# FFN heads with early tables, quartered centring and side-by-side gates, attention loops written out, and matmuls without a reader

## The reference

```
x = x + 0.5 * ffn(layernorm(x))
x = x + attention(layernorm(x))     # 16 heads of 32, causal
x = x + 0.5 * ffn(layernorm(x))

ffn(x):  gate = x @ Wg.T ; up = x @ Wu.T          # Wg, Wu: 4096 x 512
         out = (gelu_tanh(gate) * up) @ Wd.T      # Wd: 512 x 4096
layernorm(x) = (x - mean) / sqrt(var + 1e-5)
```

## Time and profile before

| | |
|---|---|
| median of three runs | 2982.96 us (2982.94 to 2984.21) |
| the profiled execution | 2983.2 us |
| its span, first to last instruction | 2981.4 us |
| TensorE busy | 2904.1 us (97%) |
| VectorE busy | 1826.8 us (61%) |
| ScalarE busy | 1052.5 us (35%) |
| GpSimd busy | 1069.3 us (36%) |
| mean granted clock of TensorE | 0.991 |
| packets of the instruction queue | 115, 1.88 MB |

### The profile page before, as it was taken

One profiled execution on the slowest core, in us unless ns is written; L12 is line 12 of the kernel. 1 busy time (PEld: TensorE's weight loads), 2 busy tenths in 40 slices (PEclk: granted clock), 3 DMA queues, 4 the chain that ended last, 5 costly groups with the idle time before them and its releaser, 6 DMA issues. The chain is left out here.

```text
span 2981.4 us, 51041 instructions
## 1 busy us (share of the span) xinstructions
PE 2904.1 (97%) x19280; PEld 2342.2 (79%) x19280; DVE 1826.8 (61%) x3312; ACT 1052.5 (35%) x1825; POOL 1069.3 (36%) x745
## 2 busy tenths in 40 slices
PE   6999999999999999999999999899999999999999
PEld 5888888888888878777777776678888888888887
DVE  5656665565666544576777675675656665565654
ACT  4322222222222222266666664432222222222222
POOL 3322222222222224466666663342222222222221
PEclk9999999999999999999999999999999999999999
DMA  3001000000000015722322222100000000000001
GB/s 99 27 24 29 21 28 21 21 25 25 28 21 28 1 47 113 220 72 59 71 59 63 68 75 71 39 29 22 26 25 28 21 28 21 21 24 26 28 8 57
DMA packets 98586, 127.95 MB, mean 43 GB/s; under 512 B 43020, under 2 KB 51196, under 8 KB 95100
## 3 DMA queue, kind: packets, MB, share of 16 engines
q1 hardware_dynamic: 98428, 125.72, 15.3%
HBM read 96.34 MB, written 29.34 MB: 42 GB/s over the span
## 5 line engine op out<-in xcount | busy, mean ns | idle before, releaser
L59 PE MATMUL psum<-ffn_x_high,ffn_w_high 128*128 128x512 f32 x2048 | 801.6, 391 | 16.7 <-POOL ffn_x_low L212 9.5
L60 PE MATMUL psum<-ffn_x_low,ffn_w_high 128*128 128x512 f32 x2048 | 798.0, 390 | 0.0
L61 PE MATMUL psum<-ffn_x_high,ffn_w_low 128*128 128x512 f32 x2048 | 798.0, 390 | 0.0
L589 POOL TENSOR_TENSOR ffn_inner<-ffn_gelu,ffn_inner 128x512 fp32r<-128x512 f32 x256 | 345.6, 1350 | 1169.1 <-ACT ffn_inner L527 1169.1
L434 DVE SCALAR_TENSOR_TENSOR ffn_gelu<-ffn_gelu,psum 128x512 f32<-128x512 f32 x256 | 176.0, 687 | 604.1 <-ACT ffn_gelu L520 604.1
L59 PEld LDWEIGHTS psum<-ffn_x_high,ffn_w_high 128*128 128x128 f32 x2048 | 385.0, 188 | 105.4 <-POOL ffn_x_low L212 10.0
L61 PEld LDWEIGHTS psum<-ffn_x_high,ffn_w_low 128*128 128x128 f32 x2048 | 385.0, 188 | 80.1
L60 PEld LDWEIGHTS psum<-ffn_x_low,ffn_w_high 128*128 128x128 f32 x2048 | 385.2, 188 | 79.0
L59 PE MATMUL psum<-ffn_inner,ffn_w_high 128*128 128x512 f32 x1024 | 398.6, 389 | 0.2
L60 PE MATMUL psum<-ffn_inner,ffn_w_high 128*128 128x512 f32 x1024 | 398.4, 389 | 0.0
L61 PE MATMUL psum<-ffn_inner,ffn_w_low 128*128 128x512 f32 x1024 | 398.4, 389 | 0.0
(11 more groups left out here) (120 smaller groups left out, 3520.5 us busy)
## 6 DMA issues: line engine op xcount, KB each, us to landing
ffn_words<-packed SPq DMA_DIRECT2D x96, 256.0 KB
ffn_word_scales<-scales SPq DMA_DIRECT2D x96, 256.0 KB
qk_parts<-parts SPq DMA_DIRECT2D x32, 512.0 KB, 3.9
queries<-qk_parts SPq DMA_DIRECT2D x48, 256.0 KB, 4.3
keys<-qk_parts SPq DMA_DIRECT2D x48, 256.0 KB, 6.2
x<-x_in SPq DMA_DIRECT2D x4, 1024.0 KB, 15.3
v_parts<-parts SPq DMA_DIRECT2D x16, 256.0 KB, 3.2
values<-v_parts SPq DMA_DIRECT2D x16, 256.0 KB, 7.0
```

What stands on the lines that cost most here:

```text
L59: pe.matmul(out, w_high, x_high, start=first, stop=False, skip_group_check=True)
L60: pe.matmul(out, w_high, x_low, start=False, stop=False, skip_group_check=True)
L61: return pe.matmul(out, w_low, x_high, start=False, stop=last, skip_group_check=True)
L589: pool.tensor_tensor(inner[:, tb % 2, m, 1, :], product[m], f32(inner[:, tb % 2, m, 0, :]), ALU.subtract)\
```

## The change

- `NormConstants` gets a one-column tile `root`, `load_root_table` (a Sqrt of it on ScalarE) and `keep_warm` (matmuls of 128x128 on constants into a bank that nobody reads).
- The first norm of each FFN: `keep_warm` of 1 behind the sums, 5 behind the spreading of the mean, 1 behind each of the first three pieces of the variance and 6 behind it; in the first FFN 4 more ahead of the sums. The root's table is asked for at the start of ScalarE's stream in both FFNs and in the projection.
- Block 0 of x comes with four DMAs of one piece, each with a semaphore, and its centring is four instructions; `square` waits for each piece.
- `first_gates` makes both gate tiles of block 0 piece by piece (24 matmuls) ahead of the variance of block 1; before, one tile stood ahead of it and one behind.
- For block 2 the spreading of the inverse stands ahead of a gate, the inverting ahead of centring 3, and scaling, high and low ahead of gelu of tile (1,0).
- The attention loops of TensorE and ScalarE are written out, as those of the other engines are.

```diff
+    def load_root_table(self, act):
+        act.activation(self.root[:], self.eps[:], ACT.Sqrt)
+
+    def keep_warm(self, pe, bank, matmuls):
+        for _ in range(matmuls):
+            pe.matmul(bank[:, 0:P], self.spreaders[:, 0, :], self.spreaders[:, 1, :], start=True, stop=True,
+                      skip_group_check=True)
...
     def sums(self, pe, tb):
-        if self.x_loaded is not None:
-            pe.wait_ge(self.x_loaded[tb], 16)
         if tb >= 2:
-            pe.wait_ge(self.centred_ready, tb - 1)
+            pe.wait_ge(self.centred_ready, KT * (tb - 1))
         for k in range(KT):
+            if self.x_loaded is not None:
+                pe.wait_ge(self.x_loaded[tb][k], 16)
             last = self.quarter_sums(pe, self.mean_bank[tb % 2], self.x[:, k, cols(tb, TB)], k)
...
-        dve.tensor_tensor(self.centred[tb % 2], self.x[:, :, cols(tb, TB)],
-                          self.mean_bank[tb % 2].unsqueeze(1).broadcast_to([P, KT, TB]),
-                          ALU.subtract).then_inc(self.centred_ready, 1)
+        if tb == 0:
+            for k in range(KT):
+                dve.tensor_tensor(self.centred[0][:, k, :], self.x[:, k, cols(0, TB)], self.mean_bank[0],
+                                  ALU.subtract).then_inc(self.centred_ready, 1)
+        else:
+            dve.tensor_tensor(self.centred[tb % 2], self.x[:, :, cols(tb, TB)],
+                              self.mean_bank[tb % 2].unsqueeze(1).broadcast_to([P, KT, TB]),
+                              ALU.subtract).then_inc(self.centred_ready, KT)
...
     def square(self, act, tb):
-        act.wait_ge(self.centred_ready, tb + 1)
         if tb >= 1:
             act.wait_ge(self.variance_ready, tb)
         for k in range(KT):
+            act.wait_ge(self.centred_ready, KT * tb + k + 1)
...
             if x_in is not None:
-                sp.dma_start(x[:, :, cols(0, TB)], x_in[:, :, cols(0, TB)]).then_inc(x_loaded[0], 16)
+                for k in range(KT):
+                    sp.dma_start(x[:, k, cols(0, TB)], x_in[:, k, cols(0, TB)]).then_inc(x_loaded[0][k], 16)
...
+            def first_gates():
+                pe.wait_ge(w_low_ready, GATE + 1)
+                for k in range(KT):
+                    pe.wait_ge(n.low_ready, k + 1)
+                    c, b = divmod(k, 2)
+                    for m in range(2):
+                        w = slice(c * GROUP + m * P, c * GROUP + (m + 1) * P)
+                        split_products(pe, gate_bank[m], w_high[0][:, b, GATE, w], w_low[0][:, b, GATE, w],
+                                       x_high[:, k, cols(0, TB)], x_low[:, k, cols(0, TB)], k == 0, k == KT - 1)
...
             if x_in is not None:
                 constants.wait(pe)
+                constants.keep_warm(pe, up_bank[1], 4)
             n.sums(pe, 0)
+            constants.keep_warm(pe, up_bank[1], 1)
             n.spread_mean(pe, 0)
-            n.variance(pe, 0)
+            constants.keep_warm(pe, up_bank[1], 5)
+            n.variance(pe, 0, warm_bank=up_bank[1])
+            constants.keep_warm(pe, up_bank[1], 6)
             n.spread_inverse(pe, 0)
             n.sums(pe, 1)
             n.spread_mean(pe, 1)
-            gate_up_part(0, 0, 0, 0, GATE, first=True, norm=True)
+            first_gates()
             n.variance(pe, 1)
-            gate_up_part(0, 0, 0, 1, GATE, first=True)
...
             n.spread_mean(pe, 3)
+            n.spread_inverse(pe, 2)
             gate_up_part(0, 0, 1, 1, GATE)
-            n.spread_inverse(pe, 2)
...
+            n.invert(dve, 2)
             n.centre(dve, 3)
-            n.invert(dve, 2)
+            n.scale(dve, 2)
             gelu_tiles(0, 0, 1, [0])
-            n.scale(dve, 2)
...
+            constants.load_root_table(act)
             n.take_mean(act, 0)
...
             n.take_mean(act, 3)
+            n.high(act, 2)
             gelu_tiles(0, 0, 1, [0])
-            n.high(act, 2)
...
             gelu_tiles(0, 0, 0)
+            n.low(pool, 2)
             gelu_tiles(0, 0, 1, [0])
-            n.low(pool, 2)
...
-            with pe.Fori(0, HEADS // 3) as hp:
+            for hp in range(HEADS // 3):
                 for s in range(3):
                     head(hp, s)
...
-            with act.Fori(0, HEADS // 3) as hp:
+            for hp in range(HEADS // 3):
                 for s in range(3):
                     head(hp, s)
```

More of the change, by code:

```diff
@@ L84, in __init__ @@
         self.std = ctx.enter_context(nc.sbuf_tensor("std", [P, P], F32))
+        self.root = ctx.enter_context(nc.sbuf_tensor("root", [P, 1], F32))
         self.ready = ctx.enter_context(nc.semaphore("constants_ready"))
@@ L111, in __init__ @@
         self.mean, self.std = constants.mean, constants.std
+        self.constants = constants
         self.mean_bank, self.var_bank = mean_bank, var_bank
@@ L170, in square, with variance @@
         for k in range(KT):
+            act.wait_ge(self.centred_ready, KT * tb + k + 1)
             act.activation(self.squares[:, k, :], self.centred[tb % 2][:, k, :], ACT.Square)\
                .then_inc(self.squares_ready, 1)
-    def variance(self, pe, tb):
+    def variance(self, pe, tb, warm_bank=None):
         if tb >= 2:
@@ L179, in variance @@
             last = self.quarter_sums(pe, self.var_bank[tb % 2], self.squares[:, k, :], k)
+            if warm_bank is not None and k < KT - 1:
+                self.constants.keep_warm(pe, warm_bank, 1)
         last.then_inc(self.variance_ready, 1)
@@ L254, in ffn @@
         product = [gelu[:, 4 + n, :] for n in range(2)]
-        x_loaded = [sem(f"x_loaded{tb}") for tb in range(NTB)] if x_in is not None else None
+        x_loaded = None
+        if x_in is not None:
+            first_loaded = [sem(f"x_loaded0_{k}") for k in range(KT)]
+            x_loaded = [first_loaded] + [[sem(f"x_loaded{tb}")] * KT for tb in range(1, NTB)]
         n = Norm(nc, ctx, tag, x, x_high, x_low, [centred0[:, :, :], centred1[:, :, :]],
@@ L293, in _ @@
                 for tb in range(1, NTB):
-                    sp.dma_start(x[:, :, cols(tb, TB)], x_in[:, :, cols(tb, TB)]).then_inc(x_loaded[tb], 16)
+                    sp.dma_start(x[:, :, cols(tb, TB)], x_in[:, :, cols(tb, TB)]).then_inc(x_loaded[tb][0], 16)
             with sp.Fori(1, NGROUP) as g:
@@ L309, in _, with gate_up_part @@
         def _(pe):
-            def gate_up_part(gg, s, tb, m, piece, first=False, norm=False):
-                if not first and piece == GATE:
+            def gate_up_part(gg, s, tb, m, piece, norm=False):
+                if piece == GATE:
                     pe.wait_ge(product_ready, 16 * gg + (8 * s + 2 * tb + m - 1))
@@ L477, in _ @@
             gelu_tiles(0, 0, 0, [1], first=True)
+            n.invert(dve, 2)
             n.centre(dve, 3)
-            n.invert(dve, 2)
+            n.scale(dve, 2)
             gelu_tiles(0, 0, 1, [0])
-            n.scale(dve, 2)
-            dve.wait_ge(n.centred_ready, NTB)
+            dve.wait_ge(n.centred_ready, KT * NTB)
             dve.wait_ge(n.normed_ready, KT * (NTB - 1))
```

## The result

| | before | changed |
|---|---|---|
| median | 2983.05 us (4 runs, 2982.94 to 2984.21) | 2958.38 us (4 runs, 2955.45 to 2961.43) |
| ratio of the changed to before | | 0.9917, 95% interval 0.9899 to 0.9934 |
| profiled execution's span | 2981.4 us | 2957.3 us |
| forecast | | 2948.9 us, range 2945.0 to 2958.0 |

What follows compares the result with a forecast made beforehand. TensorE bounds the kernel; only removing its pauses or lower-clock time helps. Loops 23.7, first FFN 6.6 and second FFN 3.8 sum to 34.1 us: 2983.0 - 34.1 = 2948.9 us, range 2945.0 to 2958.0.

Steps and rivals of the forecast that it cites:

- The loop term: Attention loops of TensorE and ScalarE written out: four turns between passes vanish, pauses and slow clock together, saving 23.7 us.
- every boundary inside a pass has the same work: Attention: head boundaries inside a pass give other engines a turn's work yet take 34.11 us, so all 23.7 is gained.
- something else is late next: Attention, lower bound: only the issue pauses go and another wait replaces them at the turns, gaining 13.4 us.
- The first FFN: Head of the first FFN: 5.4 us from the earlier up matmuls plus 1.2 from block 2's second tile, 6.6 gained.
- I cost this at nothing, up to 1 if that cover is gone: First FFN: three more DMA issues delay words and later x blocks by 1.8 us, costing nothing, at most 1.
- The second FFN: Head of the second FFN: up matmuls 2.6 us sooner plus 1.2 in its second half, 3.8 gained.
- First gate 1.9 sooner: Second FFN: warm spreading and next sums bring the first gate 1.9 us sooner after its first sums.
- The projection: Root table asked for early in the attention's projection: saves nothing visible, bounds 0 and 1.3 us.
- (c): Rival: straight attention code makes TensorE wait at fetches; pauses at every fourth packet cost 57 us, giving 3006; chance 0.02.
- (a): Rival: low clock through the first gates eats both FFN heads' gain; only the loops count, 2959.3 us; chance 0.11.
- (b): Rival: attention pauses are not the loop's; only the FFN heads gain, 10.4 us, giving 2972.6; chance 0.04.
- (d): Rival: all 34 added matmuls lie on the path, costing 17.7 us of the gain, giving 2966.6; chance 0.02.

## Why the prediction was wrong

**The loop term** (23.7, range 22.7 to 24.7) was mis-sized: it measured 19.4. Its argument on TensorE held: the turns went away whole, there is no pause at a fetch, and with ScalarE's stream kept or its waits swapped the fourteen heads take 478.1 to 478.3 us, 23.0 to 23.2 less than before. The step that failed is "every boundary inside a pass has the same work ... and takes 34.11. So I take the whole 23.7": it took the rate of a head from a kernel in which ScalarE ran a loop, and costed nothing for writing that loop out. The order of two waits there made each head 0.26 us longer, 3.6 us over fourteen. The other 0.7 us of the term is heads of 34.15 for 34.11, which no run explains. The prediction's own bound for "something else is late next" was 13.4, and 19.4 lies inside it; its range took 22.7 as the least without a reason.

**The first FFN** (6.6, range 3 to 8) measured 5.6, 6.2 and, with all parts and block 1 in time or nearly, 6.9 to 7.6. The steps held: inverse at 16.39, its spreading warm, first gate for the forecast 21.6 at 21.2 to 21.4 where both blocks were in time or nearly, and at 21.7 and 21.9 in two profiles in which the last piece of block 0 landed 0.4 and 0.6 us later; side by side gives 0.8 and block 2's order 1.6 (forecast 1.2). The step at fault is "I cost this at nothing, up to 1 if that cover is gone": it was gone in four profiles of nine, for up to 1.83 us, and once the clock fell behind it. That nobody had waited for block 1 was taken for its being in time: the trace of before has it landing at 19.7, when the prediction needed it at about 18. The three more issues put it back by 0.9 us (asked for at 6.30 for 5.40), not 1.8.

**The second FFN** (3.8) measured 2.9 in the first profile and 4.1 to 4.5 in the others that have all parts of the new heads; the 2.9 is the fall of the clock that the prediction had named and not taken. "First gate 1.9 sooner" was exact where the clock held: 14.31 for 16.23.

**The projection** (0, bounds 0 to 1.3 of gain) is the step whose bounds lay on one side only: it lost 1.7. The early table brought no gain, as forecast; what I did not count was that the rest of the change moves the instruction packets of everything behind it.

**The rivals.** (c), fetches as pauses of TensorE, did not happen; a fetch did cost time, but in a data transfer. (a), (b) and (d) are refuted by the heads' 7.4 and 4.5, by the run with TensorE's loop alone, and by the warm matmuls being worth 1.8 us in each FFN.

**The clock's timing** moves each profile by 1 to 2 us, which the range had not allowed for outside the FFN heads; the last head's 1.4 in the forecast's account is that. With the waits swapped and the squares first the kernel takes 2948.56 us and its projection 170.55, as before's. That this is the forecast's 2948.9 is in part luck: beside the order of the waits and the late landing it also has the new order of the DMAs, its second FFN gained 0.7 more than forecast and its last head lost 1.5.

## What to carry to other kernels

Before writing out an engine's loop, ask it of each engine apart, and price a pass of the straight code on the engines that had no turn to lose. A transfer that nobody waits for need not be in time for a kernel that asks sooner: read its landing. Where an instruction has two waits, see which of them ends up in an instruction of its own, and let that be the one which is satisfied first. When added instructions are costed, look at which transfers and waits lie far behind them: keep work that is ready ahead of a copy that waits for a landing.

## What the runs showed of the hardware

- Where an exp on ScalarE had a wait instruction of its own ahead of it that ended last, it started 0.061 to 0.062 us behind that instruction's start, and TensorE's head was 0.26 us longer by six of them.
- A turn of the same loop cost between 39.2 - 34.1 = 5.1 and 40.95 - 34.1 = 6.8 us, depending on the kernel around it.
- One packet of the instruction queue, 0.9 to 1.7 us long, inside a 1 MB transfer went with a landing 0.6 to 1.4 us later, the last packets of the transfer one behind another; 19 matmuls added to TensorE's stream 1070 us earlier decided whether it fell inside.
- The granted clock can stay at 1.00 through a pause of 1.9 us and fall behind the next: the same code took 84.7 or 86.1 to 86.3 us.
